# Two attention heads on the two row halves of TensorE, one maximum and one exponential for both, and a new placing of the side work

## What is computed

```
probs = softmax(x @ w_router.T);  gate, idx = top_k(probs.T, cap = 98)      # per image and expert
h     = experts' first layer on the chosen tokens, summed back to tokens     # 196 x (768 + 3*192)
x_mlp, q, k, v = split(h)                                                    # q, k, v: 12 heads of 16
attn  = softmax(q @ k.T * 16**-0.5) ;  x_attn = attn @ v                     # per head, 196 x 196
y2    = concat(gelu(x_mlp), x_attn)
out   = x + gated second layer of y2 (768 + 192 -> 192)
```

## Time and profile before

| | us |
|---|---|
| median of 3 runs (1749.19 to 1767.99) | 1757.34 |
| the profiled execution | 1757.22 |
| its span in the profile | 1755.4 |
| PE busy in the span | 1517.8 |
| DVE busy | 1218.5 |
| ACT busy | 847.3 |
| POOL busy | 248.9 |
| mean granted clock of PE, share of 2.4 GHz | 0.939 |

### The profile page before, as it was taken

How to read it: one execution, slowest core, us unless ns; L and a number is a source line. 1 busy time by engine, 2 the same in 40 slices (tenths; PEclk the granted TensorE clock), 3 DMA queues, 4 the chain that set the end, 5 groups by cost and what they waited for, 6 DMA issues and landing times.

```text
span 1755.4 us, 34644 instructions
## 1 busy us (share of the span) xinstructions
PE 1517.8 (86%) x12440; PEld 1258.9 (72%) x12440; DVE 1218.5 (69%) x2824; ACT 847.3 (48%) x1934; POOL 248.9 (14%) x319
## 2 busy tenths in 40 slices
PE   2146889898998999988998899989899989999998
PEld 2033778687786878777786777778687778878786
DVE  6658678757887578766887488765787677563552
ACT  0002555455554465454554555545554555546653
POOL 3021012200211002200111002300022002110000
PEclk9986889889999899998999899999899999989999
DMA  8985665516662475615673366706655152102220
GB/s 228 241 205 159 164 159 149 144 42 159 170 184 60 110 180 150 163 34 144 162 181 95 86 161 171 187 15 158 145 151 145 38 147 51 35 19 60 50 53 15
DMA packets 99574, 218.02 MB, mean 124 GB/s; under 512 B 61359, under 2 KB 75853, under 8 KB 88654
## 3 DMA queue, kind: packets, MB, share of 16 engines
q10 hardware_dynamic: 12032, 150.94, 32.4%
q1 hardware_dynamic: 87374, 64.88, 16.4%
HBM read 186.57 MB, written 28.90 MB: 123 GB/s over the span
## 4 chain that ended last, share of the span: by engine, by line
PE 50%; DVE 24%; issue 13%; DMA 7%; POOL 3%; ACT 2%; SPq 0%; DVEq 0%; POOLq 0%; ACTq 0%
PE bank L1050 12%; DVE psums L1258 9%; DVE peaks L1458 6%; PE bank L955 6%; PE bank L1019 5%; PE bank L985 5%; PE bank L1004 4%; DMA xt<-in_x_dram 4%; DMA qs<-shiftT 3%; PE bank L967 3%; POOL var L1590 2%; PE bank L878 2%; PE bank L1028 2%; PE bank L829 2%; PE bank L942 2%
## 5 line engine op out<-in xcount | busy, mean ns | idle before, releaser
L1458 DVE TENSOR_REDUCE peaks<-bank 98x2 f32<-98x392 f32 x768 | 423.3, 563 | 173.4 <-PE bank L985 152.7
L1207 ACT ACTIVATE Pb<-bank 98x392 f32<-98x392 f32 x768 | 374.5, 497 | 301.8 <-PE bank L1004 253.3
L1258 DVE TENSOR_REDUCE psums<-xt 112x2 f32<-112x512 f32 x672 | 425.8, 677 | 39.0 <-DMA xt<-in_x_dram 20.8
L1050 PE MATMUL bank<-w2T,hid 128*98 128x192 f32 x1536 | 312.1, 343 | 0.0
L985 PE MATMUL bank<-ks,qs 96*98 96x196 f16 x1536 | 269.3, 262 | 41.8 <-DVE peaks L1458 37.3
L1004 PE MATMUL bank<-qs,ks 97*98 97x196 f16 x1536 | 269.0, 259 | 23.3 <-DMA qs<-shiftT 21.5
L985 PEld LDWEIGHTS bank<-ks,qs 96*98 96x98 f16 x1536 | 166.1, 128 | 132.0 <-DVE peaks L1458 65.2
L1050 PEld LDWEIGHTS bank<-w2T,hid 128*98 128x98 f32 x1536 | 249.9, 176 | 3.6
L1004 PEld LDWEIGHTS bank<-qs,ks 97*98 97x98 f16 x1536 | 167.7, 130 | 35.4 <-DMA qs<-shiftT 24.4
L1019 PE MATMUL bank<-Pb,vals 98*32 98x196 f32 x3072 | 172.6, 343 | 1.2 <-ACT Pb L1207 1.2
L1618 POOL TENSOR_TENSOR fin<-fin,both 98x384 f32<-98x384 f32 x64 | 63.9, 998 | 728.8 <-DVE fin L1483 728.8
(11 more groups left out here) (185 smaller groups left out, 1777.9 us busy)
## 6 DMA issues: line engine op xcount, KB each, us to landing
xt<-in_x_dram ACTq DMA_DIRECT2D x94, 1568.0 KB, 9.0
qk_scratch<-qk SPq DMA_DIRECT2D x64, 294.0 KB, 4.1
qs<-qk_scratch SPq DMA_DIRECT2D x192, 73.5 KB, 3.0
ks<-qk_scratch SPq DMA_DIRECT2D x192, 73.5 KB, 3.1
out_dram<-fin SPq DMA_DIRECT2D x64, 147.0 KB
xt<-in_x_dram SPq DMA_DIRECT2D x2, 1568.0 KB, 15.3
qs<-shiftT SPq DMA_DIRECT2D x128, 2.3 KB
hid<-in_L_ffn_w_dram SPq DMA_DIRECT2D x1, 1440.0 KB
```

The lines of the kernel that those rows point to most:

```text
L1050: mm = pe.matmul(misc_ps[slot][0:HT, D * h:D * h + D], lhs, w2T[0:w, f, :], start=(f == 0), stop=(f == NF + 1))
L1207: act.activation(Pb[:, (H * i + h) % NP, :, :].rearrange("p a b -> p (a b)"), score_ps[s][0:HT, 0:2 * T], ACT.Exp, scale=float(DH) ** -0.5 ...
L1258: last = dve.tensor_reduce(psums[:, m % 2, t, 2 * p:2 * p + 2], v[:, 2 * p:2 * p + 2, :, :], AX.XY, ALU.add)
L1458: dve.tensor_reduce(peaks[:, h // 6, :, h % 6], peak_ps[s][0:HT, 0:2 * T].rearrange("p (q k) -> p q k", q=2), AX.X, ALU.max, negate=True). ...
```

## The change

- `KS` becomes 48 (three blocks of 16 rows, no zero rows). The heads of an image are laid in pairs: one on partitions 0 to 48, the other from partition 64 (`ODD`) to 112. `qs` and `ks` are [128, 3, 6, 196] instead of [97, 3, 12, 196]. The rows of ones come from two memsets; the memsets of `qs` and of the whole of `ks` go.
- `peak` and `score` do nothing at odd h. At even h they do both heads: for each half of the queries or keys one matmul of the low rows and one of the high rows, in turn, into two neighbouring banks. One semaphore counts both.
- DVE reduces the two banks at once (98 x 784 to 98 x 4), ACT takes one exponential over both.
- `qk16`, `qk_scratch`, the columns of `M` and `peaks` get the order that goes with it. `stack` issues eight DMAs instead of six, with the same bytes; `shift` two instead of one.
- `fc2` stands in slots 0, 3, 6, 7, 8, 9 instead of 4 to 9.
- `TAKE` is 22 instead of 25, `routing` in the body is two slots longer, `rounds` gives each slot a credit of at least 0.65, `chosen` and `spread` stand one slot later behind the last round and `turning` half a slot; `quiet` ends four slots behind the last round. The tables' costs of peak and score are lower.
- `planes` and `tok` of the next group come 5 slots behind their pooling instead of 3.5; those of the third pair of images go from the end of `opening()` to slots 2 and 4 of the next body. In the opening, side work goes in front of the peaks.

```diff
-KS = 96
+KS = 3 * DH
+ODD = 64
+FC2_SLOTS = (0, 3, 6, 7, 8, 9)
...
-        credit = min(credit + cost(TENSOR, plan[at]) - cost(VECTOR, plan[at]), 2)
+        credit = min(credit + max(cost(TENSOR, plan[at]) - cost(VECTOR, plan[at]), 0.65), 2)
...
-TAKE = 25
-VECTOR = {"peak": 0.52, "choose": 1.05, "first_max": 0.52, "take": 0.9, "norm1_scale": 0.9, "norm1": 0.8, "shift1": 1,
+TAKE = 22
+VECTOR = {"peak": 0.45, "choose": 1.05, "first_max": 0.52, "take": 0.9, "norm1_scale": 0.9, "norm1": 0.8, "shift1": 1,
...
-TENSOR = {"peak": 0.35, "score": 0.35, "mix": 0.65, "fc2": 0.89, "hidden": 2, "project": 1.33, "values": 0.66,
+TENSOR = {"peak": 0.19, "score": 0.19, "mix": 0.65, "fc2": 0.89, "hidden": 2, "project": 1.33, "values": 0.66,
...
-                fill[4 + k] = [("fc2", 0, i - 1, k)] + fill[4 + k]
+                fill[FC2_SLOTS[k]] = [("fc2", 0, i - 1, k)] + fill[FC2_SLOTS[k]]
...
-    front, at = routing(1, TAKE)
+    front, at = routing(1, TAKE, 2)
     for slot, op in in_slots(front):
         plan[slot].append(op)
-    quiet = (int(at), H * GRP)
-    at = rounds(plan, 1, int(at))
-    for slot, op in in_slots(choosing(1, at + 1) + turning(1, at + 4)):
+    began = int(at)
+    at = rounds(plan, 1, began)
+    quiet = (began, at + 4)
+    for slot, op in in_slots(choosing(1, at + 2) + turning(1, at + 4.5)):
         plan[slot].append(op)
     pieces = TILES * PIECES
     at = evenly(plan, pieces * (GRP // PAIR - AHEAD), 0, TAKE - 4)
-    front = []
+    front = [(2, ("planes", 1, AHEAD - 1)), (4, ("tok", 1, AHEAD - 1))]
...
-            front += pooling(2, m, at[pieces * m:])
+            front += pooling(2, m, at[pieces * m:], behind=5)
     for slot, op in in_slots(front):
-        plan[min(slot, len(plan) - 1)].append(op)
+        if op[0] in ("planes", "tok") and op[1:] == (2, AHEAD - 1):
+            continue
+        into = plan[min(slot, len(plan) - 1)]
+        peaks_at = [k for k, other in enumerate(into) if other[0] == "peak"]
+        into.insert(peaks_at[0] if slot >= H * GRP and peaks_at else len(into), op)
...
+                for m, st in enumerate((qs, ks)):
+                    for c in range(2):
+                        both_ = qk_dram[i % 2, c, m].rearrange("s d w -> (s d) w")
+                        low = ODD * c
+                        sp.dma_start(st[low:low + 2 * DH, s, :, :].rearrange("d h t -> d (h t)"), both_) \
+                            .then_inc(stack_in[s], 16)
+                        sp.dma_start(st[low + 2 * DH:low + KS, s, :, :].rearrange("d h t -> d (h t)"),
+                                     both_[DH * (1 - m):DH * (1 - m) + DH, :]).then_inc(stack_in[s], 16)
...
             def peak(at, G_, dg, i, h):
-                s = h % 2
+                if h % 2:
+                    return
...
-                pe.wait_ge(peak_free[s], 6 * (GRP * G_ + i) + h // 2 + ONE)
+                pe.wait_ge(peak_free, 6 * (GRP * G_ + i) + h // 2 + ONE)
                 for q in range(2):
-                    mm = pe.matmul(peak_ps[s][0:HT, T * q:T * q + T],
-                                   qs[0:KS, i % NSTACK, h, HT * q:HT * q + HT], ks[0:KS, i % NSTACK, h, :],
-                                   start=True, stop=True)
-                mm.then_inc(peak_full[s], 1)
+                    for s in range(2):
+                        mm = pe.matmul(peak_ps[0:HT, s, T * q:T * q + T],
+                                       qs[ODD * s:ODD * s + KS, i % NSTACK, h // 2, HT * q:HT * q + HT],
+                                       ks[ODD * s:ODD * s + KS, i % NSTACK, h // 2, :], start=True, stop=True)
+                        if q == 1:
+                            mm.then_inc(peak_full, 1)
...
                 for k in range(2):
+                    for s in range(2):
+                        mm = pe.matmul(score_ps[0:HT, s, T * k:T * k + T],
+                                       ks[ODD * s:ODD * s + KS + 1, i % NSTACK, h // 2, HT * k:HT * k + HT],
+                                       qs[ODD * s:ODD * s + KS + 1, i % NSTACK, h // 2, :], start=True, stop=True)
+                        if k == 1:
+                            mm.then_inc(score_full, 1)
...
-                act.activation(Pb[:, (H * i + h) % NP, :, :].rearrange("p a b -> p (a b)"), score_ps[s][0:HT, 0:2 * T],
-                               ACT.Exp, scale=float(DH) ** -0.5).then_inc(score_free[s], 1)
+                act.activation(Pb[:, at_:at_ + 2, :, :].rearrange("p s a b -> p s (a b)"), score_ps[0:HT, :, 0:2 * T],
+                               ACT.Exp, scale=float(DH) ** -0.5).then_inc(score_free, 1)
...
-                dve.tensor_reduce(peaks[:, h // 6, :, h % 6],
-                                  peak_ps[s][0:HT, 0:2 * T].rearrange("p (q k) -> p q k", q=2),
-                                  AX.X, ALU.max, negate=True).then_inc(peak_free[s], 1)
+                dve.tensor_reduce(peaks[:, h // 6, :, :, h % 6 // 2].rearrange("p q s -> p s q"),
+                                  peak_ps[0:HT, :, 0:2 * T].rearrange("p s (q k) -> p s q k", q=2),
+                                  AX.X, ALU.max, negate=True).then_inc(peak_free, 1)
```

More of the change, by code:

```diff
@@ L169, in rounds, with routing @@
     return at
[L172 to L176 removed]
+def routing(dg, at, wide=0):
+    ops = [(at, ("take", dg)), (at + 1, ("norm1_scale", dg))]
+    at += wide / 2
+    ops += [(at + 3.5, ("norm1", dg)), (at + 4.5, ("norm1_turn", dg)), (at + 5.5, ("norm1_key", dg)),
+            (at + 6.5, ("own_image", dg, 0, 0))]
     at += 7.5
@@ L239, in prologue @@
     plan = [in_order(front + turning(0, at + 0.5 * ROUNDS + 3))] + opening(0, False)
-    for slot, op in in_slots(pooling(1, 2, steadily(1, 0.24))):
-        plan[min(slot, len(plan) - 1)].append(op)
+    for slot, op in in_slots(pooling(1, AHEAD - 1, steadily(1, 0.24))):
+        if op[0] not in ("planes", "tok"):
+            plan[min(slot, len(plan) - 1)].append(op)
     return sum(plan, [])
@@ L494, in bass_vit_tower @@
         w2T = sb("w2T", [128, NF + 2, D])
-        banks = [ctx.enter_context(nc.psum_tensor(f"bank{b}", [128, 512], F32)) for b in range(8)]
-        score_ps = banks[0:2]
-        peak_ps = banks[2:4]
-        misc_ps = banks[4:8]
+        score_ps, peak_ps = (ctx.enter_context(nc.psum_tensor(f"{n_}_ps", [128, 2, 512], F32)) for n_ in ("score", "peak"))
+        misc_ps = [ctx.enter_context(nc.psum_tensor(f"misc{b}", [128, 512], F32)) for b in range(MISC)]
+        banks = [score_ps[:, 0, :], score_ps[:, 1, :], peak_ps[:, 0, :], peak_ps[:, 1, :]]
         qk_dram = nc.dram_tensor("qk_scratch", (2, 2, 2, 2, DH, H // 2 * T), F16, kind="Internal").ap()
@@ L728, in shift @@
                 sp.wait_ge(shift_ready, 2 * n_ + part + 1)
-                sp.dma_start(qs[KS:KS + 1, i % NSTACK, 6 * part:6 * part + 6, :],
-                             shiftT[:, part, :]).then_inc(shift_in[part], 16)
+                for c in range(2):
+                    sp.dma_start(qs[ODD * c + KS:ODD * c + KS + 1, i % NSTACK, 3 * part:3 * part + 3, :],
+                                 shiftT[3 * c:3 * c + 3, part, :]).then_inc(shift_in[part], 16)
             def fc2(at, G_, dg, i, k):
@@ L1013, in mix @@
                     pe.wait_ge(vals_ready, GRP * G_ + i + 1)
-                for s in range(2):
-                    pe.wait_ge(score_free[s], 6 * (GRP * G_ + i) + 2 * c + 2 + ONE)
+                pe.wait_ge(score_free, 6 * (GRP * G_ + i) + 2 * c + 2 + ONE)
                 for q in range(2):
@@ L1193, in project @@
                     act.wait_ge(misc_full[slot], k + 1)
-                    act.copy(qk16[:, m, 0, :, :].rearrange("p c t -> p (c t)"), misc_ps[slot][0:DC, 0:2 * T]) \
+                    act.copy(qk16[:, :, 1 + m, :], misc_ps[slot][0:DC, 0:2 * T].rearrange("p (c t) -> p c t", c=2)) \
                         .then_inc(hi_ready, 1)
```

90 lines of the change are left out of this document (39 added, 51 removed).

## The result

The changed kernel takes 1817.43 us (median of 4 runs, 1802.31 to 1825.71), beside 1761.93 of the kernel before (4 runs): a ratio of 1.0315, 95% interval 1.0219 to 1.0411. It is slower by 3.2%, where 1690 us was forecast with a range that ended at 1780. The profiled execution took 1812.71 us, with a mean granted clock of 0.908 where 0.939 stood before.

What follows compares the result with a forecast made beforehand. TensorE was taken to bound the kernel, with VectorE close behind. From 1757 us, 18 for the paired heads, 8 for the joint reduction and 41 for the placing were subtracted, giving 1690 us, range 1615 to 1780.

Steps and rivals of the forecast that it cites:

- Part 1, the two halves: Peak and score matmuls of two heads overlap on TensorE's row halves: a joint block takes 0.66 us against 0.68.
- Rival A: Rival: the two row halves don't overlap on TensorE; 1820 us, chance 0.09.
- D: Rival: entering and leaving the row-half form is cheap or hidden behind waits; 1578 us, or 1634 half hidden; chance 0.15.
- the sum of -18: TensorE's net gain from heads side by side: 2.3 us a group, -18 us over eight; bounds -130 and +112.
- Rival C: Rival: TensorE becomes thin and its mean clock falls to 0.85, giving back 70 us; 1760 us, chance 0.15.
- Part 2, one maximum and one exponential: One reduction on VectorE (0.94 us) and one exponential on ScalarE (at most 0.99) per pair: -8 us and 0.
- The -8 for the waits: VectorE, busy 58 us less, shortens TensorE's waits for it by 8 us; bounds 0 and -58.
- rival B: Rival: a pair has no second bank, costing 0.35 us a pair; 1832 us if all pay, 1743 a third; chance 0.10.
- B's sign: What would show rival B: VectorE idle before the peaks' reduction as often as there are pairs.
- Part 3: New placing of rounds, planes and second layer: waits for chosen rows and planes go, -41 us.
- The second layer in slots 0, 3, 6 to 9 is the same matmuls: 0: Spreading the second layer's slots changes nothing, 0 us, though one ring bank is held longer; bounds -10 and +10.
- the -41 for `chosen`, planes and rounds: Waits at chosen rows and planes and the half clock behind them: 69 us at most, -41 taken; bounds 0 and -69.

Runs made afterwards that it cites:

- e2: The change's paired heads under the whole old placing of the kernel before: 1781.65 us, 1.0110 of the kernel before.
- m2: e2 with peak reductions reading only 24 of every 196 columns (maxima not right): 0.9637 of the kernel before, 0.9593 when run again.
- e3: Kernel before with two heads' full-width matmuls sharing one wait, reduction and exponential, both banks freed together: 1783.67 us, 1.0140 of the kernel before.
- n1: Kernel before with five of seven pooling additions left out: 1708.55 us, 0.9705 of the kernel before.
- n3: e3 with five of seven pooling additions left out: 1727.59 us, 0.9816 of the kernel before.
- e9: e7 with the routing started at slot 25 again and without its two extra slots: 0.9802 of the kernel before, 0.9771 when run again.
- m1: Kernel before with peak reductions reading only 24 of every 196 columns (maxima not right): 1683.73 us, 0.9592 of the kernel before.
- m3: e3 with peak reductions reading only 24 of every 196 columns (maxima not right): 1688.91 us, 0.9599 of the kernel before.
- e4: The changed kernel with the second layer back in slots 4 to 9: 1781.93 us, 1.0105 of the kernel before.
- e1: Heads of the kernel before under the whole new placing of the change: 1771.61 us, 1.0082 of the kernel before.
- e5: Old heads and old peak and score costs under the new placing, but second layer in slots 4 to 9: 1742.59 us, 0.9896 of the kernel before.
- e6: The changed kernel with one part of the second layer moved from slot 3 to slot 5: 1797.36 us, 1.0211 of the kernel before.
- e7: e5 without the credit floor of 0.65 in the rounds: 1740.13 us, 0.9899 of the kernel before.
- e8: e7 with the opening's side work behind its peaks and planes 3.5 slots behind the pooling again: 1753.81 us, 0.9987 of the kernel before.
- e10: The placing of e9 with the change's paired heads: 1732.05 us, 0.9848 of the kernel before.
- n2: e2 with five of seven pooling additions left out: 1726.31 us, 0.9808 of the kernel before.

## Why the prediction was wrong, by its own steps

**Part 1, the two halves.** The price of a block was right. In the timeline of the kernel after:

```profile
705.96 0.91 PE L871 MATMUL misc<-aT,tm 128*98 128x196 f32 x4
706.79 0.37 PE L996 MATMUL peak_ps<-ks,qs 48*98 48x196 f16 x4
707.00 0.33 PE L1018 MATMUL score_ps<-qs,ks 49*98 49x196 f16 x4
707.26 1.22 PE L1064 MATMUL misc<-w2T,hid 128*98 128x192 f32 x6
708.32 0.83 PE L871 MATMUL misc<-aT,tm 128*98 128x196 f32 x4
```

Four peak matmuls need 0.21 us until the next block starts (0.17 forecast), and four scores 0.26. The last matmul ahead of such a block needs 0.26 us instead of 0.17, and the first behind it 0.24 instead of 0.16. (The 0.83 us of the first row are 0.08 longer than that, because its first matmul came late.) That is 0.47 + 0.09 + 0.08 = 0.64 us a block against the 0.66 of the forecast and the 0.68 of full width. Rival A (no overlap) is out. So is D: entering and leaving cost 0.30 us over the 0.34 of the stream, as the mix had shown. The Trainium skill (TensorEngine Tiling (Array Packing), Key Properties) has a change of mode drain TensorE; this trace agrees, with 0.09 us on entering and, on leaving, 0.09 in the last score and 0.08 in the matmul behind it. The last group came 3.5 us shorter, where I had it within 3 of its old length.

The step that failed is that the sum of -18 held the granted clock still. The halves shorten the steps by 6.5 us a group (e2), more than the 2.3 forecast. (Blocks that follow one another directly, or stand ahead of a mix, change form once where I had counted twice; the rest of the difference was not worked out.) But the half clock adds 8.4 us a group, as TensorE's time at half clock goes from 21 us to 45, and that term was at nothing. Rival C had named it, with a mean clock of 0.85 that was not reached (0.89), and it was priced too low: a mean of 0.85 is some 61 us at half clock in a group of 202, 40 more than before, and at e2's rate (8.4 us for 24 more) that is 14 us back, not 9. Where the reduction is short (m2), the steps give 5.6 us a group, the half clock takes 4.2 and waits 2.9, and the halves' gain is gone there too.

**Part 2, one maximum and one exponential.** The reduction takes 972 ns (0.94 forecast), the exponential 823 (at most 0.99 forecast), DVE's busy time fell by 31 us over all (58 was forecast from the reductions alone, which fell by 49.9). The -8 for the waits was wrong in sign: they rose from 37.3 us to 62.9 (e2). The step that failed is that the loss of the second bank was left out of the sum and kept as rival B at 0.10, on the ground that "most have poolings or rounds between". Poolings between don't protect a pair: in e3's timeline two of them make its reduction late. Nor are they the root, since with most of them gone (n1 to n3) the pair costs 1.1% still. B's sign, DVE idle before the reduction as often as there are pairs, didn't show either: DVE waited there 130 times for 384 pairs, and 165.6 us in all (173.4 before). It is PE that stands. Where the placing is the old one or e9's, the heads as a whole cost 14 to 25 us (0.8 to 1.4% of 1757), where -26 was forecast; m1 to m3 show that this cost goes when the reduction is short.

**Part 3.** "The second layer in slots 0, 3, 6 to 9 is the same matmuls: 0", bounds -10 and +10, failed by most: +35 us (e4), 33 by e1 against e5. I asked what bank it holds and not what it had covered. e6 puts some 20 us of it on one part. Of the -41 for `chosen`, planes and rounds, e5 gives -1.04%, some 18 us. The waits for the planes in the loop went, and those for the chosen rows fell from 19.6 to 6.0 us; but the waits for peaks rose from 37.3 to 66.1 us. "Where PE stops waiting, DVE is soon last" was in the text. The routing's earlier start, which I had put at 0, with bounds of 0 and -12, cost 1% of the kernel or a little more (e7 against e9). Without it the same part gives -2.0 to -2.3% (e9), 35 to 40 us. That this is close to the -41 of the forecast is in part luck, since the hidden layer's 16.9 us of waits are in it and were not in the sum.

**The sum by what was measured**, in ratios: the heads +1.1% (e2), the spread second layer +1.9%, the earlier routing +1.0%, the later planes and the order in the opening -0.9%, and the rest of Part 3 about -1.1% (e8, without these and with the earlier routing, stands at 0.9987). That is +2.0%, and 3.2% were measured. The 1.2% between show up wherever the new heads meet the routing's new place: on the new heads the whole placing without the spread gives nothing (e4 1.0105, e2 1.0110), on the old ones 1.0%, while in e9's placing it gives 2.6% on the new heads (e10) and 2.0 to 2.3% on the old. So they lie in what separates e4 from e10, and the half clock is where they appear in the trace (7.4 us a group against 3.3). Whether the routing alone does it, or the tables' costs have a share, and why the clock falls more often there, was not tested.

## What to carry to other kernels

Joining two small operations into one takes the two buffers that stood between producer and consumer and makes one of them: before joining, count whether the producer can still run ahead by the length of the longest thing in the consumer's queue. A piece of independent work in an in-order list is also the cover of the latencies on either side of it; before moving it, name the results that are in flight over its place. And a saving in the bounding engine's streaming is only a saving if the clock holds: read the granted clock with it. What a change costs can hang on what stands beside it: the same pair cost 0.8% in one placing and 2.1% in another.

## What the runs showed of the hardware

- Matmuls on the two row halves start 3 to 4 ns apart and the next two 0.08 us later (0.12 for the first two of a block), and four of 48 rows took 0.21 us to the next block. The change of form costs 0.09 us on entering and 0.17 on leaving. The Trainium skill (TensorE: Matmul & The Clock Gate, Part 3) has weights for other row groups loaded during matmuls; the near-equal starts agree with it.
- A maximum over 98 x 784 took 972 ns, 98 x 392 took 563, and 98 x 48 still took 206. By these three, an estimate, about 0.16 us of a reduction doesn't depend on its length. The exponential goes from 497 to 823 ns on doubling.
- The shift row's DMA of 1.1 KB (2.3 KB before) was waited for until 6.2 to 9.3 us after its issue, in the kernel before and after alike, with one exception of 2.6 us.
- With matmuls on row halves the granted clock is lower at about the same busy time of PE: n1 and n2 have PE busy 906 and 904 us over the five groups, at 0.95 and at 0.91. The halves do less in that time at full clock; what in their pattern lowers the clock was not tested.
